# The first layer's weights fetched in two transfers of 512 KB a batch instead of four of 256 KB

## The reference

```
# layer 0: one 512x512 matrix per batch
x = x + einsum('bsd,bdh->bsh', x, W0[cat_ids]) + b0[cat_ids][:, None, :]
# layer 1: a shared MLP, 384 output columns shared, 128 by the batch's expert
h      = gelu(einsum('bnd,hd->bnh', x, fc1_w) + fc1_b)          # 2048 wide, exact gelu
shared = einsum('bnh,sh->bns', h, fc2_w) + fc2_b
expert = einsum('bnh,bph->bnp', h, experts_w[idx]) + experts_b[idx][:, None, :]
x = x + concatenate([shared, expert], axis=-1)
```

## Time and profile before

| | |
|---|---|
| median of three runs | 1757.18 us (1754.25 to 1759.35) |
| span of the profiled execution | 1768.6 us, 26735 instructions |
| PE busy | 1714.2 us (97%) |
| DVE, ACT, POOL busy | 972.8, 583.3, 205.4 us |
| DMA | 246.13 MB, mean 139 GB/s |
| weight loads `w_raw` | 256 transfers of 256 KB, median 3.3 us from issue to landing |

### The profile page before, as it was taken

One profiled execution on the slowest core, in us unless ns is written; L12 is line 12 of the kernel. 1 busy time (PEld: TensorE's weight loads), 2 busy tenths in 40 slices (PEclk: granted clock), 3 DMA queues, 4 the chain that ended last, 5 costly groups with the idle time before them and its releaser, 6 DMA issues.

```text
span 1768.6 us, 26735 instructions
## 1 busy us (share of the span) xinstructions
PE 1714.2 (97%) x7681; PEld 1383.7 (78%) x7681; DVE 972.8 (55%) x1688; ACT 583.3 (33%) x991; POOL 205.4 (12%) x198
## 2 busy tenths in 40 slices
PE   6999999999999999999999999999999999999999
PEld 5777778788787878878787887878878787887887
DVE  6544534655555565555556565565556546555554
ACT  5444443333232333323233232333333333333321
POOL 1200100200202020020201002020110202002010
PEclk9999999999999999999999999999999999999999
DMA  8888785444535444453444435443443544445121
GB/s 272 264 255 264 237 252 154 134 104 133 134 95 147 114 130 113 121 143 92 142 130 116 110 109 150 114 143 105 139 113 107 143 116 129 107 122 147 54 66 48
DMA packets 296858, 246.13 MB, mean 139 GB/s; under 512 B 145636, under 2 KB 219508, under 8 KB 296820
## 3 DMA queue, kind: packets, MB, share of 16 engines
q1 hardware_dynamic: 277956, 211.31, 42.2%
q10 hardware_dynamic: 18864, 34.35, 6.2%
HBM read 212.02 MB, written 33.55 MB: 139 GB/s over the span
## 4 chain that ended last, share of the span: by engine, by line
PE 75%; DMA 8%; SPq 6%; DVE 5%; issue 3%; ACT 1%; POOL 1%; DVEq 0%; ACTq 0%
PE ps_out L776 33%; PE ps_h L761 18%; PE ps_e L761 14%; PE ps_y L748 7%; DMA resid<-in_L_cond_experts_b 3%; DMA turn_in<-in_L_cond_experts_w 2%; SPq L317 2%; PE ps_t L678 2%; DMA exp_t<-turn_out 2%; PE ps_e L678 2%; SPq L345 1%; DVE resid L620 1%; DVE h L561 1%; SPq L355 1%; DVE w_split L561 1%
## 5 line engine op out<-in xcount | busy, mean ns | idle before, releaser
L776 PE MATMUL ps_out<-w2e,h 128*128 128x512 f32 x3072 | 770.6, 398 | 0.0
L776 PEld LDWEIGHTS ps_out<-w2e,h 128*128 128x128 f32 x3072 | 575.4, 189 | 135.9
L761 PE MATMUL ps_h<-y_t,w 128*128 128x512 f32 x1728 | 426.9, 397 | 1.4 <-DVE y_t L561 1.4
L761 PEld LDWEIGHTS ps_h<-y_t,w 128*128 128x128 f32 x1728 | 323.0, 188 | 75.0 <-DVE y_t L561 1.6
L608 DVE CAST h<-g_raw 128x512 fp32r<-128x512 f32 x256 | 123.9, 484 | 449.2 <-ACT g_raw L508 449.2
L761 PE MATMUL ps_e<-y_t,w 128*128 128x512 f32 x1344 | 331.2, 396 | 0.0
L761 PEld LDWEIGHTS ps_e<-y_t,w 128*128 128x128 f32 x1344 | 253.4, 189 | 60.3
L480 ACT CAST w2e<-e_raw 128x512 fp32r<-128x512 f32 x224 | 139.0, 621 | 375.7 <-PE ps_out L776 375.7
L748 PE MATMUL ps_y<-w_split,x_t 128*128 128x512 f32 x744 | 219.5, 404 | 25.7 <-DVE x_t L561 23.0
L561 DVE TENSOR_TENSOR w_split<-w_raw,w_split 128x512 fp32r<-128x512 f32 x256 | 179.3, 701 | 79.1 <-ACT w_split L462 78.9
L601 DVE CAST w2e<-w2e 128x512 fp32r<-128x512 f32 x256 | 120.3, 470 | 141.2 <-PE ps_out L776 141.2
(11 more groups left out here) (54 smaller groups left out, 574.7 us busy)
## 6 DMA issues: line engine op xcount, KB each, us to landing
w_raw<-in_L_cond_W SPq DMA_DIRECT2D x256, 256.0 KB, 3.3
e_raw<-exp_t SPq DMA_DIRECT2D x448, 128.0 KB, 2.4
b_all<-in_L_cond_b SPq DMA_DIRECT2D x64, 256.0 KB, 3.7
turn_in<-in_L_cond_experts_w ACTq DMA_DIRECT2D x64, 256.0 KB, 4.9
exp_t<-turn_out ACTq DMA_DIRECT2D x64, 256.0 KB, 5.2
out<-resid SPq DMA_DIRECT2D x64, 256.0 KB, 2.1
x_blocks<-in_x SPq DMA_DIRECT2D x240, 64.0 KB, 2.5
x_raw<-in_x SPq DMA_DIRECT2D x60, 256.0 KB, 3.9
```

The lines of the kernel that those rows point to most:

```text
L761: last = nc.tensor.matmul(h_bank(c, direct)[:, :], w1[:, w, k, c * P:(c + 1) * P], y_t[:, a, k, :, :].rearrange("p b s -> p (b s)"), start ...
L776: last = nc.tensor.matmul(ps_out[b][:, :], h[:, c % 2, a, b * S:(b + 1) * S], fc2_columns(c, c % 2, w, b), start=(c == 0 and n == 0), stop ...
```

## The change

`load_l0` issues a transfer only for slices 0 and 2 of a batch, and it carries two slices: 128 partitions x 2 x 2 KB = 512 KB into two neighbouring slots of `w_raw`. It waits until both slots are free, so for an even slice `j` until slice `j - 3` has been read instead of `j - 4`. The two slots of a pair share one semaphore, and `w_high` waits on the pair's. All that is computed stays the same, and so do the bytes. The lines behind L328 move down by one, so L345 is L346 and L355 is L356 afterwards.

```diff
-        w_in = [sem(f"w_in{i}") for i in range(WSLOTS)]
+        w_in = [sem(f"w_in{i}") for i in range(WSLOTS // 2)]
...
-                after(sp, w_lo, G * NC + b * KD + k - WSLOTS + 1)
-                sp.dma_start(w_raw[:, k, :], l0_w[bass.ds(load_l0.cat, 1), k * P:(k + 1) * P, :]
-                             .rearrange("o d n -> (o d) n")).then_inc(w_in[k], 16)
+                if k % 2 == 0:
+                    after(sp, w_lo, G * NC + b * KD + k + 1 - WSLOTS + 1)
+                    sp.dma_start(w_raw[:, k:k + 2, :], l0_w[bass.ds(load_l0.cat, 1), k * P:(k + 2) * P, :]
+                                 .rearrange("o (t d) n -> (o d) t n", t=2)).then_inc(w_in[k // 2], 16)
...
-                after(act, w_in[j % WSLOTS], 16 * (G * (NC // WSLOTS) + j // WSLOTS + 1))
+                after(act, w_in[j % WSLOTS // 2], 16 * (G * (NC // WSLOTS) + j // WSLOTS + 1))
```

## The result

The changed kernel takes 1766.69 us, the median of 15 runs (1758.76 to 1770.68), and the kernel before, on the same chip, 1759.05 us (1754.25 to 1762.66). The ratio of the mean times is 1.0037, with a 95% interval of 1.0025 to 1.0049: slower, by 6.5 us (the two medians lie 7.6 us apart). The prediction said 1761.1 us, 3.9 us more than before, in a range of 1753 to 1772 us, with "no change" (0.55) as the likeliest verdict and "slower" (0.38) next to it.

What follows compares the result with a forecast made beforehand. PE was taken as the bound, with 54.4 us idle, and in the loop the path of SP's issues and the expert bias's landing. 13 groups x 0.30 us = 3.9 us on 1757.2 gave 1761.1 us, range 1753 to 1772.

Steps and rivals of the forecast that it cites:

- no change: Whole kernel: measured time between 1751.9 and 1762.5 us, a difference too small to tell; chance 0.55.
- The place in the queue: Loop: slice of step 5, 256 KB, now goes ahead of the expert bias and delays it, 0.22 us a group.
- the prologue: First groups: odd slices come earlier, slice 12 up to 2.7 us late; ends -3 and +3 us, taken as 0.
- The fixed part of the transfers: Loop: the fixed part of 128 transfers goes, but nobody waits for those slices, so worth nothing there.
- The issue on SP: Loop: a pair's issue ahead of the bias takes about 0.08 us more than a single slice's, +0.08 us a group.
- The queue: Loop: the 256 KB slice now queued ahead of the expert bias makes it land later, 0.22 us a group.
- the backlog passes whole: Rival, loop: bias loses all of 1.04 us a group, plus three groups at lower clock: 1775.5 us; chance 0.25.
- a wait under 20 us: Sign, loop: PE's `x_t` wait under 20 us would mean the 256 KB behind the bias had slowed it.
- The signs that I had named: No ACT wait for `w_raw` behind 40 us; PE's busy time in the first 40 us near 28.2 us.
- The later wait in the loop: Loop: even slices wait one slice later, one step less of lead, adding nothing ahead of the bias; cost 0.
- PE's clock: After a long wait PE runs slower, 1.6 us a group where it happens; no further groups counted.
- Large transfers pay: Rival: odd slices arrive with partners, ACT's weight waits go, at most 6.3 us won: 1750.9 us; chance 0.10.

Runs made afterwards that it cites:

- experiment 7: Kernel before, with only slice 5 in the loop issued next to slice 4, ahead of the expert biases: 1759.06 us, ratio 0.9999.
- experiment 11: Kernel before with expert biases issued right behind the stores and pairs in the loop only: 1736.35 us, ratio 0.9858.
- before again: Second profile of the unchanged kernel before, no edit: span 1757.3 us, timed 1760.19 us, ratio 1.0000.
- experiment 12: Kernel before with a useless 512 KB transfer right behind slice 4, ahead of the expert bias, in every loop group: 1775.74 us, ratio 1.0074.
- experiment 8: Kernel before with the expert biases issued right behind the stores in step 4: 1732.89 us, ratio 0.9845.
- Experiment 3: Kernel before with pairs in the early groups 0 to 2 only, single slices in the loop: 1767.09 us, ratio 1.0040.
- experiment 10: Kernel before, with only slices 12 and 14 of group 0 waiting for one slice more: 1763.88 us, ratio 1.0016.
- experiment 5: Kernel before, one transfer a slice in its old place, but even slices wait as the pair does: 1763.99 us, ratio 1.0021.
- experiment 6: Changed kernel with single slices for the last four of group 0 and the first four of group 1: 1763.57 us, ratio 1.0023.
- the order alone: Changed kernel's order and wait, but each pair as two 256 KB transfers issued together: 1769.45 us, ratio 1.0047.

## Why the prediction was right and wrong

The direction and the range held, and the size within a factor of 1.7 (3.9 forecast, 6.5 measured). That is luck: the loss comes from elsewhere. The likeliest verdict, "no change", didn't come, and 1766.69 us is above the forecast's own range of 1758 to 1765. Two steps failed. "The place in the queue", the term that was to decide, is nil as far as can be measured (experiment 7). And the prologue, put at 0, makes PE some 3 us late by 57 us; further early losses and the clock, counted as none, are the likely rest.

**The fixed part of the transfers: 0.** Held. Single transfers in the pairs' order cost as much as the pairs do (1.0047 against 1.0037), and pairs bring nothing where the bias is out of the way (experiment 11).

**The issue on SP: +0.08 us a group.** Wrong in place. One group of the kernel after, answering to the earlier trace rows:

```profile
952.99 0.42 SPq L329 DMA_DIRECT2D w_raw<-in_L_cond_W  x1
...
956.48 1.88 SPq L356 DMA_DIRECT2D resid<-in_L_cond_experts_b  x4
...
962.23 1.01 POOL L439 TENSOR_TENSOR resid<-y,b_all 128x384 f32<-128x384 f32 x1 [35.82 <-DMA resid<-in_L_cond_experts_b]
...
963.79 0.69 DVE L591 TENSOR_TENSOR y<-ps_y,x_raw 128x512 f32<-128x512 f32 x1 [2.20 <-POOL resid L440]
...
967.88 0.95 PE L749 MATMUL ps_y<-w_split,x_t 128*128 128x512 f32 x3 [1.19 <-DVE x_t L562]
```

A pair's issue takes 0.38 to 0.39 us mostly (forecast 0.40 to 0.45), but the one ahead of the bias takes 0.42, and the single one there had taken 0.41 too. Laid against the same matmul of PE, SP's bias issue comes at the same time within 0.03 us in 12 groups of a trace: 0.14 us later than before again in the kernel after, but 0.02 with pairs in the loop alone and 0.17 with early pairs alone, where the loop has single slices. So the 0.14 us aren't the pair's issue; what they are is open. A second issue (experiment 7) makes it 0.52 us.

**The queue: +0.22 us a group.** Wrong; it is nil as far as can be measured. From issue to POOL's start the mean of 13 groups is 5.92 us after, 5.88 before again and 6.17 in the first profile; I had said 6.5. Single profiles differ in it: of the five that have slice 5 ahead of the bias it is 5.62 (experiment 7) to 6.28 (pairs in the loop alone), 5.94 on average, and of the five that have it behind 5.88 to 6.17, 5.96 on average. The 1.34 us between the last group (4.83, and after 1679.47 to 1683.97) and the others, which I had divided by bytes, is thus not a price by bytes: another 512 KB (experiment 12) makes the mean 6.01 us, 0.13 more than before again, and delays the issue by 0.49 us. The sum, 0.62, is near PE's 0.66 us. So even there the delay is mostly SP's issue time. But where the bias stands does count: issued right behind the stores, ahead of the blocks of `x`, the weights and the expert slices (experiment 8), it takes 4.76 us on average, about as in the last group. The rule of ring order of the Trainium skill ("DMA: Bandwidth & Descriptors", section on queues, rings and completion order) is not against this, if what was ahead had gone before the bias came; the gaps of the earlier trace rows allow it, and no run shows it. The rival "the backlog passes whole" falls with it, since PE's wait did not grow. By the sign that I had named, a wait under 20 us, the 256 KB behind the bias would have been what slowed it; but before again has 18.6 us with these 256 KB in place, so the 18.0 don't say that.

**The prologue: 0, "what one transfer gains another loses".** This is where the other step failed. Inside the prologue it even held: ACT waits 6.4 us for weights in the first 40 us after, 6.3 before, and the casts of slices 12 and 13 wait for no transfer (the pair goes at 28.84, since slice 9 is cast at 26.40 and not at 28.32). But I had weighed only the slice that waits, and of what stands behind it on SP I had asked only in the loop. At the seam SP issues with next to no gap, and the DMA engines are busy for 0.84 of the first 40 us; of the 2.9 us that the expert slices are late, 2.4 reach the first weights of group 1 and 2.8 is what PE's first slice of group 1 is late. Experiment 3 shows that the loss is early (1.0040), the table that it is there by 57 us (3.3 us between the means of the unchanged kernels and of the five with the whole late wait), and experiment 10 that two late waits are enough for a part (1.0016, just clear of 1). It is not the whole: experiment 5 has a delay of its own, and experiment 6 keeps half of the delay without these waits. The signs that I had named don't settle it: ACT does wait for weights behind 40 us, but so it does in five kernels with the old early order, and PE's 27.28 us of work in the first 40 lie within what those show (26.66 to 28.78).

**The later wait in the loop: 0.** As far as can be told, it held: from matmul 1280 to the end the kernel after gains 0.4 us on before again, and its windows are alike. The timed ratio of loop pairs alone, 1.0017 (1.0003 to 1.0031), says 0.5 to 5.5 us for all that pairs do in the loop.

**PE's clock: none counted.** That was too little. At the seam PE starts again at half clock, and the three L749 alone lose 0.7 us. Up to 1690 us PE spends 17.0 us at the lower level in the trace of after and 10.2 in before again. The timed runs say the same: the mean granted clock is 0.9945 over the 15 runs after and 0.9964 over 71 runs of the kernel before, which is up to 3.3 us of the 6.5, an estimate from the difference times the span, if PE had work all the time. Such stretches stray: the kernel with the order alone has a pause at the seam as well (3.6 us of wait in ACT) and none there. In the loop they are 6.8 us in before again and in after, 13.6 in the first profile of before, 17.0 with the order alone and 27.2 with 512 KB more, so most of what the last two lose beyond PE's waits for `x_t` can be the clock.

**"Large transfers pay".** Against it: ACT's waits for `w_raw` went up, 5.9 to 9.2 us. The rule of the Trainium skill ("DMA: Bandwidth & Descriptors", rules for kernel authors) to coalesce many small transfers, with 64 KB as the size under which one pays mostly overhead, brings nothing here at 256 KB: 1.0037 with pairs. The two slices in one transfer are not slower than in two issued together (1.0047), so the loss comes with the order and the wait, and not with the size.

**What stays open.** How the rest of the 6.5 us splits. In the kernel after and with early pairs alone PE loses another 2.3 and 2.7 us between matmuls 200 and 640, in group 0; after with the bias first, the same kernel up to there, loses 0.4, and bias first with the loop's pairs, which has no pairs there at all, 3.8. So one profile each can't tell whether pairs cost something in this stretch. The order alone loses 10 us in the loop of its one profile and slice 5 ahead of the bias only 1 to the end of the loop, though both issue the bias 0.51 us later: PE waits 24.1 and 19.5 us for `x_t`, and spends 17.0 and 6.8 us at the lower clock. Why the bias lands later in the one (5.98 and 5.62 us from issue to POOL) I can't say.

## What to carry to other kernels

A merged transfer waits for its last slot, and where the issuing engine works in order, that wait is paid by what stands *behind* it: price it at every place where the queue has no slack, the start and the seams between phases first, not only in the loop. More bytes ahead of a critical small transfer may cost little but the issuing engine's time, as here, so before a mean between two rows is divided by bytes, lay the same stretch over more rows. And a single profile may stray by 11 us of 1760: add what lies around its span, and compare with the timed runs before a term rests on its waits. Kernels that differ only further on serve as repeats: a wait that they show too is no sign of the change.

## What was not expected of the hardware

The span of one and the same kernel was 1768.6 and 1757.3 us in two profiles, and of the 11.3 us 7.6 came in the loop, with longer waits in the same 13 places (23.0 against 18.6 us on PE). SP's bias issues, in contrast, kept their distance to PE's matmuls within 0.03 us from group to group. And the bias issued at about 1480 us took 6.99 to 7.83 us to reach POOL in each of the eleven profiles that have the bias in its old place, 7.73 in the earlier trace rows, where most others lie near 5.8. The cause is open; it stays with one group, and no run here varied the data.
